# Decoder block in one program: first tile prepared over three banks, last tile's attention with two buffers, next but one tile begun at a round's end, residual by pairs

## The reference

```python
x = x + L0_attn(layernorm(x))        # gated delta rule
x = x + L0_xattn(layernorm(x), ctx)  # differential cross attention
x = x + L0_ffn(layernorm(x))         # causal conv, 8 experts (top 2), gelu ffn
```

```python
Sd   = g * S
S    = Sd + outer(k, beta * (v - k @ Sd))
o    = q @ S
out  = (rmsnorm(o) * silu(gate)) @ out_proj_W.T + out_proj_b
```

## Time and profile before

| | us |
|---|---|
| median of three runs | 1618.92 |
| profiled execution, its own time | 1627.61 |
| span of the profiled execution, first to last instruction | 1625.8 |
| PE busy | 1519.0 (93%) |
| DVE busy | 1179.9 (73%) |
| ACT busy | 830.7 (51%) |
| POOL busy | 209.2 (13%) |

### The profile page before, as it was taken

The page is one execution under the profiler, slowest core; times in us unless marked ns, Lnnn a source line. Parts: engine busy times, 40 slices in busy tenths (PEclk is TensorE's granted clock), DMA queues, the critical chain, the costliest instruction groups (busy, mean ns, idle before and its releaser), DMA issues.

```text
span 1625.8 us, 39269 instructions
## 1 busy us (share of the span) xinstructions
PE 1519.0 (93%) x16376; PEld 1024.8 (63%) x16376; DVE 1179.9 (73%) x3193; ACT 830.7 (51%) x1594; POOL 209.2 (13%) x212
## 2 busy tenths in 40 slices
PE   5899999999999999999999999999999999999898
PEld 4475676656766566656766566656766577757764
DVE  6267769775987679785888669785888677955653
ACT  1354354654555564654565564654555554543333
POOL 0030111002200021001200021001300022101000
PEclk7999999999999999999999999999999999999999
DMA  5010000000100001000100000000100001000000
GB/s 219 1 27 27 3 20 8 29 1 14 28 27 2 2 23 18 28 1 15 27 28 2 1 28 15 28 1 15 27 14 2 1 15 28 16 1 15 1 1 13
DMA packets 20215, 31.32 MB, mean 19 GB/s; under 512 B 1480, under 2 KB 17864, under 8 KB 19784
## 3 DMA queue, kind: packets, MB, share of 16 engines
q1 hardware_dynamic: 20040, 28.82, 6.1%
HBM read 20.41 MB, written 8.39 MB: 18 GB/s over the span
## 4 chain that ended last, share of the span: by engine, by line
PE 72%; DVE 22%; ACT 3%; issue 3%; POOL 0%; DVEq 0%; ACTq 0%
PE bank L1808 14%; PE bank L1756 6%; PE bank L1530 5%; PE bank L1416 5%; PE bank L1746 4%; PE bank L1459 4%; PE bank L1732 4%; PE four L1615 4%; PE bank L1441 3%; PE bank L1531 2%; PE four L1634 2%; PE bank L1523 2%; PE four L1683 2%; DVE qkv L1038 2%; PE bank L1422 2%
## 5 line engine op out<-in xcount | busy, mean ns | idle before, releaser
L1808 PE MATMUL bank<-w_sb,cs 128*128 128x512 f32 x512 | 246.9, 602 | 0.0
L521 POOL TENSOR_TENSOR decayed<-state,pk 128x512 f32<-128x512 f32 x64 | 74.4, 1163 | 925.5 <-DVE state L1167 925.5
L797 ACT ACTIVATE cs<-bank 128x512 f32<-128x512 f32 x128 | 76.2, 596 | 172.0 <-PE bank L1422 149.1
L1808 PEld LDWEIGHTS bank<-w_sb,cs 128*128 128x128 f32 x512 | 95.1, 191 | 90.9 <-issue 80.1
L1459 PEld LDWEIGHTS bank<-c_sb 128*128 128x128 f32 x1056 | 134.2, 200 | 24.8 <-issue 17.8
L1364 DVE SCALAR_TENSOR_TENSOR cs<-cs,rwt 128x256 f32<-128x256 f32 x224 | 98.7, 482 | 70.2 <-ACT cs L797 70.1
L1459 PE MATMUL bank<-c_sb 128*128 128x128 f32 x1056 | 140.3, 286 | 5.0 <-DMA c_sb<-in_consts 5.0
L1756 PE MATMUL bank<-vx_sb,cs 128*128 128x136 f32 x1024 | 134.0, 283 | 6.3 <-ACT cs L751 6.3
L1756 PEld LDWEIGHTS bank<-vx_sb,cs 128*128 128x128 f32 x1024 | 125.2, 190 | 22.7 <-ACT cs L751 14.5
L751 ACT COPY cs<-bank 128x512 f32<-128x512 f32 x128 | 74.7, 584 | 116.7 <-PE bank L1746 115.8
L1530 PE MATMUL bank<-hT,w_sb 128*128 128x512 f32 (+1 forms) x224 | 109.7, 613 | 6.2 <-ACT pre L598 4.0
(11 more groups left out here) (240 smaller groups left out, 2954.7 us busy)
## 6 DMA issues: line engine op xcount, KB each, us to landing
xt<-in_x SPq DMA_DIRECT2D x8, 512.0 KB, 5.0
vscr<-qkv SPq DMA_DIRECT2D x8, 512.0 KB, 2.9
vT<-vscr SPq DMA_DIRECT2D x32, 128.0 KB, 4.6
Tm<-in_x SPq DMA_DIRECT2D x8, 512.0 KB, 4.1
out<-cs SPq DMA_DIRECT2D x8, 512.0 KB, 2.9
w_sb<-in_weights SPq DMA_DIRECT2D x1, 3656.0 KB, 17.9
w_sb<-in_weights SPq DMA_DIRECT2D x1, 1456.0 KB, 8.5
cs<-in_scratch SPq DMA_DIRECT2D x3, 256.0 KB, 8.6
```

The lines of the kernel that those rows point to most:

```text
L1808: mm(dst, x1T[:, k, b * TB:b * TB + TB], ew[:, k, ep * 512:ep * 512 + 512], start=k == 0, stop=False)
```

## The change

Four things are changed together, and the tables of order and of useless products are new for all engines.

1. *Three banks for the first tile.* For tile 0 the preparation steps go to banks 7, 4 and 5 in the order of the table FIRST; for other tiles still to bank 7.
2. *Two buffers in the last tile's attention.* In the second half of tile 7 the scores of odd units go to banks 0 and 1, the second turn of a unit to bank 3, `pv` to bank 2, and the probabilities of odd units lie in mk.
3. *Next but one tile.* A third mark, *, is for tile i+2: `ln1`, `turn1`, `rot` and `gate.0` of it stand at the end of round i; there is a round -2, with these for tile 0. The DVE recurrence `scan` is a step apart from `rot.1`. `sum.0` and `sum.1` of the next tile stand at the round's end too. The gate buffer sgs has five slots for it.
4. *Residual by pairs.* The gating `og`, the projection `wo` and the residual `x1` are done for two batches at a time, each with its event. xpand lies in pre instead of Tm, so `spread` doesn't wait for `x1`.

```diff
-            used = [None]
+            used = {}
+            def free(n):
+                if n in used:
+                    name, *at = used[n]
+                    pe.wait_ge(ev[name].sem, ev[name].at(*at))
...
+                def emptied(*step):
+                    here[0] = 7 if i else FIRST[step]
+                    free(here[0])
+                    return bank[here[0]]
...
+FIRST = {("turn1", 0): 7, ("turn1", 1): 4, ("rot", 0): 5, ("rot", 1): 7, ("gate", 0): 4, ("unrot",): 5, ("gate", 1): 7, ("cond",): 4, ("db",): 5,
+         ("proj", 0): 7, ("btr",): 4, ("brep", 0): 5, ("proj", 1): 7, ("brep", 1): 4, ("proj", 2): 5, ("proj", 3): 7, ("proj", 4): 4, ("proj", 5): 5}
...
-        xpand = Tm[:, 0:2, :, :].rearrange("p a b c -> p (a b c)")
+        xpand = pre[:, 3, :, :].rearrange("p b t -> p (b t)")[:, 0:512]
...
+        def scores(j, u, a):
+            return bank[a if j == NI - 1 and u % 2 else 4 + a]
+        def turned_bank(j, n):
+            return bank[3 if j == NI - 1 and n else 6]
+        def values_bank(j):
+            return bank[2 if j == NI - 1 else 6]
...
                 def pt(m):
                     u, n = m // 2, m % 2
                     up("pexp", u + 1)
-                    if n:
+                    if j == NI - 1:
+                        if u:
+                            up("pt_sb", m - 1)
+                        elif n == 0:
+                            up("qx_sb", 2)
+                    elif n:
                         up("pt_sb", m)
...
-                    up("og")
-                    for p in range(2):
-                        last = pair_to_tokens(p, bank[2 + p][:, :], kn, wo)
-                    fin("wo_ps", last)
+                    p = k - 1
+                    up("og", k)
+                    fin("wo_ps", pair_to_tokens(p, bank[2 + p][:, :], kn, wo))
...
-                    if i:
-                        pool.wait_ge(ev["x1"].sem, ev["x1"].at(i - 1))
+                    if i:
+                        pool.wait_ge(ev["mkq"].sem, ev["mkq"].at(i - 1, 8))
...
-KEEP = {(-1, -1, "mo", 0): 10, (-1, -1, "moe", 13): 9, (-1, -1, "moe", 18): 1, (-1, -1, "moe", 7): 8, (-1, -1, "pt",
+KEEP = {(-1, -1, "ffd", 0): 4, (-1, -1, "moe", 2): 1, (-1, -1, "moe", 5): 27, (-1, -1, "pt", 1): 1, (-1, -1, "pv", 5):
```

More of the change, by code:

```diff
@@ L116 @@
     "pe": steps('''
[L117 to L126, removed]
@@ L145 @@
[L145 to L154 removed]
+        decay sum.2 grow -turn2.0 -turn2.1 -qx.0 sum.3 -sc.0.0 -qx.1 -sc.0.1 vturn raw.0 raw.1 -sc.1.0 -sc.1.1 -pt.0
@@ L578, in turn1 @@
                     up("turn1_ps")
-                    fin("turn1_a", nc.scalar.copy(hT[:, 0, :], bank[7][:, :]))
+                    fin("turn1_a", nc.scalar.copy(hT[:, 0, :], room(i, "turn1", 0)[:, :]))
                 def cond(k):
@@ L602, in gate @@
                     up("gate_ps", n + 1)
-                    fin("gate_sb", A(sg[:, n, :], bank[7][:, :], ACT.Identity, bias=L("bproj", 6 + n, 7 + n)))
+                    if i >= 3 - n:
+                        act.wait_ge(ev["og"].sem, ev["og"].at(i - 3 + n, 2))
+                    fin("gate_sb", A(sgs[:, (2 * i + n) % 5, :], room(i, "gate", n)[:, :], ACT.Identity, bias=L("bproj", 6 + n, 7 + n)))
                 def db():
@@ L748, in pt @@
                     up("pt_ps", m + 1)
-                    if u and not n:
-                        up("pv_ps", u)
-                    fin("pt_sb", nc.scalar.copy(flat(probT[:, 4 * n:4 * n + 4, :]), bank[6][:, :]))
+                    depth = 2 if j == NI - 1 else 1
+                    if u >= depth and not n:
+                        up("pv_ps", u - depth + 1)
+                    fin("pt_sb", nc.scalar.copy(flat(probT_of(j, u)[:, 4 * n:4 * n + 4, :]), turned_bank(j, n)[:, :]))
                 def asq_(p):
@@ L1210, in x1_ @@
+                def x1_(n):
+                    up("wo_ps", n + 1)
+                    if n == 0:
+                        dve.wait_ge(xres_in.sem, xres_in.at(i, 16))
+                        if i:
+                            dve.wait_ge(ev["done"].sem, ev["done"].at(i - 1, 2))
+                    fin("x1", tt(flat(xr[:, 2 * n:2 * n + 2, :]), bank[2 + n][:, :], flat(xres[:, 2 * n:2 * n + 2, :]), ALU.add))
                     assert ch.count == DVE_AB, ch.count
                     assert ch1.count == DVE_IN, ch1.count
-                return {"ln1": ln1, "turn1": turn1, "rot": rot, "unrot": unrot, "cond": cond, "conv": conv, "db": db, "btr": btr, "norm": sum_,
+                return {"ln1": ln1, "turn1": turn1, "rot": rot, "scan": scan, "unrot": unrot, "cond": cond, "conv": conv, "db": db, "btr": btr, "norm": sum_,
@@ L1236, in ln2 @@
                     if k == 0:
-                        up("x1")
+                        up("x1", p + 1)
                     layer_norm(p + 1, p, k)
                 def max_(u):
-                    sc = [bank[4 + a][:, :].rearrange("p (h n) -> p h n", h=8) for a in range(2)]
+                    sc = [scores(j, u, a)[:, :].rearrange("p (h n) -> p h n", h=8) for a in range(2)]
+                    prob = prob_of(j, u).rearrange("p (h f n) -> p h f n", h=8, f=2)
+                    depth = 2 if j == NI - 1 else 1
+                    if j == NI - 1 and u:
+                        up("psub", 2 * u)
                     step = []
@@ L1520, in gate @@
                         pe.wait_ge(ld_proj, 16)
-                    emptied()
+                    dst = emptied("gate", n)
                     for k in range(KC):
-                        last = mm(bank[7][:, :], ctrl[:, k, 768 + n * P:768 + n * P + P], hT[:, k, :], start=k == 0, stop=k == 1)
+                        last = mm(dst[:, :], ctrl[:, k, 768 + n * P:768 + n * P + P], hT[:, k, :], start=k == 0, stop=k == 1)
                     fin("gate_ps", last)
-                    used[0] = ("gate_sb", i, n + 1)
+                    leave("gate_sb", i, n + 1)
                 def controls(dst, at, n):
```

266 lines of the change are left out of this document (138 added, 128 removed), and 6 rows, old and new, of the table KEEP.

## The result

The changed kernel takes 1595.17 us (median of four runs, 1593.89 to 1595.61) against 1618.16 before in the same comparison: a ratio of 0.9855 with a 95% interval of 0.9833 to 0.9876. Repeated later: 1592.24 against 1619.10, 0.9841 (0.9800 to 0.9882). So the change saves 23 to 27 us; the forecast was 15.9, with a range down to 1586.

The account below looks back on a forecast made before the run. PE bounds the kernel after the attention; the attention is bound by a chain across engines. Terms −7 + 4.5 − 1.8 − 2.5 − 9.1 = −15.9 from the median 1618.9 give 1603 us; range for 8 in 10: 1586 to 1619.

Parts of the forecast that it names:

- First tile and round 0: Start of the kernel: three banks start tile 0's recurrence 5.6 us earlier, round 0 loses and gains steps; −7 in sum.
- Last tile: Attention of the last tile: two buffers cut most unit cycles from 6.5 to 5.1 us; −9.1 with the residual's first pair.
- rival C: Last tile: two buffers shorten nothing, max still stands ahead of av, the cycle stays 6.5; 1611.5 us, chance 0.12.
- Round 7: Round 7: decay without its wait, grow earlier, and wo and the residual by pairs; −2.5 us.
- From the attention's end on: Middle rounds after the attention: PE is full, so added steps are paid in full; +3.5 us a round.
- the norm beside the experts: Middle rounds' experts: ln1.1 on DVE ahead of m.7, partly in PE's path; +0.6 us, or +1.3 by the skill's rule.
- Attention of a middle round: Three steps leave it but the chain stays; 46.7 us, near round 7, against 48.8 without a fall: −2.1.
- The eight useless products: Attention of middle rounds: eight useless products come back, 2.2 us in PE's bound of 40.9.
- Round 6: Round 6 has no tile 8 to begin, so it keeps the gains without the price at its end; −1.8 us.
- Clock: Whole kernel: falls of the clock stay as many as now, one or so in a middle round at 1.7 us each.
- Rival B: Middle rounds slower: unfilled PE waits bring more clock falls and the round's end pays in full; 1623 us, chance 0.14.
- Rival A: Middle rounds win as well: attention 44 instead of 46.7, each of six rounds 2.5 us shorter; 1588 us, chance 0.24.

Follow-up runs that it names:

- first_one_bank: The changed kernel with bank 7 alone for the first tile's preparation, in the same order: 1617.98 us, ratio 0.9998 to the kernel before.
- no_early_start: The changed kernel with a tile's norm, turn, rot, scan and gate.0 back in the attention of the round before its own: 1664.76 us, ratio 1.0274 to before.
- vector_in_attention: The changed kernel with nine unused VectorE reductions of 128x512 added in the attention of rounds 1 to 6: 1626.05 us, ratio 1.0038 to the kernel before.
- no_products_attention: The changed kernel without the eight useless products in the attention of rounds 1 to 6: 1611.09 us, ratio 0.9951 to the kernel before.
- last_single: The changed kernel with one place for scores, probabilities, turns and values in the last tile too: 1615.70 us, ratio 0.9983 to the kernel before.
- norm_earlier_products: The changed kernel with ln1.1 ahead of m.6 and six more useless products, ahead of turn5.1 and pt.8, in rounds 1 to 6: 1614.95 us, ratio 0.9970 to before.
- products_in_attention: The changed kernel with 25 more useless products in the attention of rounds 1 to 6: 1618.29 us, ratio 0.9989 to the kernel before.

## Why the prediction was right, and where its size was off

The direction and the range were right; 16 us were forecast and 23 to 27 came. The terms of the last tile, of round 7 and of the way from the attention to the next round were right in size and cause. Of the other two, the middle rounds gave more than forecast, and what the first tile gave is known only roughly; that its two traces differ by just the forecast's amount is luck.

- *First tile and round 0*, −7 forecast, −7.4 between the two traces. The agreement is in part luck, since the kernel before without a change up to there begins round 1 at 218.9 in one trace and at 211.6 in another, and the changed kernel at 209.6 to 212.6. The parts (8.0, 8.5 and 4 make 20.5, where the prediction wrote 20.4): 16.5 forecast for the banks, about 17 by first_one_bank with its slow clock taken off; 14.8 for tile 1's steps ahead of the first `sum`, 11.1 by no_early_start. No run shows the 4 us given to the 35 useless products that went. That the parts nearly cancel is right; the sum is not known to better than several us.
- *Last tile*, −9.1 against −9.7: a cycle of 4.94 for 5.1. The single `pv` place and the `max` (rival C) held nothing up. What I had not counted is that without the two places this order loses, in most executions, another 8.8 to the clock.
- *Round 7*, −2.5 against −2.7. *From the attention's end on*, +3.5 against +3.2: PE is full there and the moved 6.5 us less the removed products are paid. The part of it that I gave to the norm beside the experts lies behind them. The Trainium skill's rule (SBUF — State Buffer, Who interferes with whom) agrees with the rows in kind, 3.38 us beside GpSimd's work and 1.37 without. The 1.3 us that the prediction worked out from it do not show: with the norm moved the round got back 0.6 of 2.
- *Attention of a middle round*, −2.1 forecast, −3.5 measured, in six rounds 8.4 us. This is the mis-sized term. The prediction's floor was round 7's stretch of before, 48.0 less a fall of 1.7, so 46.3 ("the chain stays"), and it took 46.7 (VectorE's relief was counted as 6.3 us; its busy time fell by 4.9, from 46.35 to 41.42). But that floor belongs to the old order of the lists. In the new order round 7, in which no step was moved away, takes 46.8 with a fall (1319.9 to 1366.7 above), and without one it is as long as a middle round, here in vector_in_attention, whose edit doesn't reach round 7:

```profile
1351.90:1397.20 45.30, 41.13 (x543) 34.36 (x542) 38.75 (x95) 22.87 (x46) 9.72 (x12) 1.00 0.16 36
```

So 1.0 of the missed 1.4 us is a gain that round 7 has as well; round 7 has fewer useless products there (14 for 22) and new lists for every engine, and no run parts the two.

- *The eight useless products* were charged as 2.2 us in PE's bound and as nothing in the 46.7. What the prediction lacked is that they hold the clock: without them the stretch is 49.0 at 0.90. With the steps moved and no filler the stretch gains nothing against 48.8; with the filler alone in before it is 2.8 longer. It takes both: as the rows ahead of `pt.4` read, the move leaves a wait and the filler fills it.
- *Round 6*, −1.8 against −3.7, follows from the same term: 1.4 of the 1.9 are the attention's.
- *Clock.* I assumed as many falls as before, and by the runs that held: the mean clock is 0.983 to 0.988 after, and 0.985 in the median of the 19 runs of before. The profile of before was an unlucky one (0.979, 15 falls and 68 us of slow clock; the changed kernel's has 9 and 48). Rival B came true only where the filler was taken away or put behind a wait, or where VectorE was loaded: in no_products_attention, last_single, norm_earlier_products and vector_in_attention. The rule of the Trainium skill that the prediction named (TensorE: Matmul & The Clock Gate, A second HAM failure mode) fits the trace of before, where the clock fell in the attention at 1000.3 and the longest wait ahead of it there was 0.77. no_products_attention doesn't test it, since PE waits 2.02 there.

Rival A was half of what happened: the middle rounds win too, at full clock 1.7 us a round more than forecast instead of 2.5. That was not for VectorE's relief alone; how the 3.5 us split between PE's work, VectorE's and the new order of the lists is open. products_in_attention and vector_in_attention cost 4.6 and 5.6, and no run has the new order without the move.

Open: what the early start of the next but one tile is worth by itself. By round 1 it costs 8.6 us (202.9 against 211.5), and no run here undoes it with a good order.

## What to carry to other kernels

Price filler work by the clock that it holds, not by its own duration: take it out of one stretch, and compare the granted clock and the busy time of the same instructions. Before adding it, look at what it waits for; filler behind a wait makes the gap that it was to fill. And when work is moved out of a stretch that waits in turns, look for the place where it had filled a wait: here `rot.0` had filled 2 us ahead of `pt.4`, and without filler there the stretch gained nothing.

Compare two kernels at equal granted clock, over several traces. A single stretch can agree with a forecast because one of the two executions was slow in it.
